# First routing that keeps four sequences' tokens in fifteen slot tiles, and fourteen attention steps moved among the first feed-forward's tiles

## What is computed

```python
x = x + 0.5 * ffn(layernorm(x), Wr, br, W1, b1, W2, b2)
x = x + attn(layernorm(x), wq, wk, wv, wproj, g_rms)
x = x + 0.5 * ffn(layernorm(x), Wr, br, W1, b1, W2, b2)

def ffn(x, Wr, br, W1, b1, W2, b2):        # 8 experts, 128 -> 512 -> 128, top 1
    expert_idx = argmax(xf @ Wr.T + br)
    h = relu(einsum('td,efd->etf', xf, W1) + b1[:, None, :])
    y = einsum('etf,edf->etd', h, W2) + b2[:, None, :]
    return y[expert_idx, arange(tokens)]

def attn(x, wq, wk, wv, wproj, g_rms):     # 16 heads of 8
    q, k, v = x @ wq.T, x @ wk.T, x @ wv.T
    q, k = rope(rms(q)), rope(rms(k))
    return softmax(q @ k.T * scale + 1.0) @ v @ wproj.T
```

## Time and profile before

| | |
|---|---|
| median of 3 runs | 525.54 us (523.85 to 528.15) |
| profiled execution, span of the core | 554.1 us |
| its mean granted TensorE clock | 0.921 of full |
| busy: TensorE, VectorE, ScalarE, GpSimd | 87%, 69%, 61%, 53% |
| first feed-forward in the trace | about 36 to 121 us |
| steps -20 to -7 (up to the first `max_scores`) | about 121 to 147 us |
| steps -6 to -1 | about 147 to 170 us |
| second feed-forward | from about 450 us |

### The profile page before, as it was taken

The page is one execution under the profiler, slowest core; times in us unless marked ns, Lnnn a source line. Parts: engine busy times, 40 slices in busy tenths (PEclk is TensorE's granted clock), DMA queues, the critical chain, the costliest instruction groups (busy, mean ns, idle before and its releaser), DMA issues.

```text
span 554.1 us, 13802 instructions
## 1 busy us (share of the span) xinstructions
PE 480.1 (87%) x4171; PEld 337.8 (61%) x4171; DVE 383.1 (69%) x1047; ACT 340.6 (61%) x765; POOL 291.4 (53%) x408
## 2 busy tenths in 40 slices
PE   7769999996968999999999999989428679979995
PEld 4349999972434555555555555555215348869994
DVE  5836777744786788988888888898117427857773
ACT  4126676632535788888888988867225456536661
POOL 7053455406997677676856665724730503454443
PEclk9989999999885799999999999989657979969999
DMA  7962222111000000000000000000100122123200
GB/s 216 257 239 59 73 70 66 50 30 38 18 18 21 12 7 13 7 11 13 13 7 2 2 4 2 3 1 13 55 25 1 36 53 62 54 66 88 65 29 10
DMA packets 28854, 25.10 MB, mean 45 GB/s; under 512 B 5683, under 2 KB 26074, under 8 KB 28272
## 3 DMA queue, kind: packets, MB, share of 16 engines
q1 hardware_dynamic: 24240, 15.75, 9.7%
q0 software_dynamic: 4544, 8.49, 5.3%
HBM read 14.65 MB, written 10.22 MB: 45 GB/s over the span
## 4 chain that ended last, share of the span: by engine, by line
PE 68%; DVE 13%; issue 6%; another core or an unknown queue 5%; ACT 4%; DMA 2%; POOL 1%; DVEq 1%; SPq 1%; POOLq 0%; ACTq 0%
PE PS L680 13%; PE PS L693 12%; PE PS L822 11%; PE PS L785 10%; DVE Smax L1476 6%; PE PS L770 5%; PE PS L755 4%; PE PS L807 2%; PE PS L852 2%; ACT QkT L909 2%; PE PS L670 1%; PE PS L832 1%; PE PS L840 1%; PE PS L795 1%
## 5 line engine op out<-in xcount | busy, mean ns | idle before, releaser
L1476 DVE TENSOR_REDUCE Smax<-PS 128x4 f32<-128x1024 f32 x128 | 156.2, 1223 | 64.6 <-PE PS L785 49.3
L1010 ACT ACTIVATE Pt<-PS 128x1024 f32<-128x1024 f32 x128 | 128.4, 1033 | 12.6 <-remote 9.4
L680 PE MATMUL PS<-XsT,Ws 128*128 128x128 f32 x624 | 92.4, 293 | 4.1 <-issue 3.3
L693 PE MATMUL PS<-W,HsT 128*128 x624 | 87.5, 285 | 4.0 <-DVE Ys L1371 3.2
L785 PE MATMUL PS<-QkT 24*128 24x256 f32 x512 | 66.0, 336 | 28.8 <-DVE Smax L1476 22.4
L950 ACT ACTIVATE HsT<-PS,Bs 128x128 f32<-128x128 f32 x156 | 48.9, 364 | 64.6 <-PE PS L680 57.6
L680 PEld LDWEIGHTS PS<-XsT,Ws 128*128 128x128 f32 x624 | 79.3, 199 | 8.5 <-issue 4.3
L693 PEld LDWEIGHTS PS<-W,HsT 128*128 128x128 f32 x624 | 78.0, 196 | 7.7 <-issue 6.5
L785 PEld LDWEIGHTS PS<-QkT 24*128 24x128 f32 x512 | 41.9, 198 | 66.4 <-ACT QkT L909 26.9
L822 PE MATMUL PS<-Pt,Vg 128*32 128x256 f32 x1024 | 77.4, 416 | 2.4 <-issue 2.0
L1357 DVE TENSOR_SCALAR HsT<-PS,Bs 128x128 f32<-128x128 f32 x156 | 47.5, 346 | 36.8 <-PE PS L680 34.0
(11 more groups left out here) (190 smaller groups left out, 698.1 us busy)
## 6 DMA issues: line engine op xcount, KB each, us to landing
AtCol<-slots SPq DMA_DIRECT2D x39, 65.5 KB, 1.8
mid<-Ys SPq DMA_DIRECT2D x39, 64.0 KB
rows<-XX SPq DMA_DIRECT2D x8, 288.0 KB, 4.2
XX<-x SPq DMA_DIRECT2D x8, 256.0 KB, 4.6
W<-w1T SPq DMA_DIRECT2D x2, 1024.0 KB, 6.5
W<-w2T SPq DMA_DIRECT2D x2, 1024.0 KB
QkT<-NmaxT SPq DMA_DIRECT2D x64, 4.0 KB
Xs<-rows,TokI POOLq DMA_INDIRECT x39
```

The costliest lines, as they stand in the source:

```text
L680: last = nc.tensor.matmul(PS[:, 2 + 2 * (n % 2) + c // 2, (c % 2) * P:(c % 2 + 1) * P], Ws[:, n % R_WS, c * P:(c + 1) * P], XsT[:, n % 2, ...
L693: last = nc.tensor.matmul(PS[:, y_bank(n), 0:P], HsT[:, n % 2, c, :], W2[:, ds(e * D_FF + c * P, P)], start=(c == 0), stop=(c == FC - 1))
L1010: nc.scalar.activation(Pt[:, m % 2, 2 * pair:2 * pair + 2, :, :].rearrange("p h c t -> p (h c t)"), PS[:, score_bank(m, pair):score_bank(m ...
L1476: nc.vector.tensor_reduce(Smax[:, b % 2, :, at:at + 33:32].rearrange("p t h -> p h t"), PS[:, max_bank(m, pair):max_bank(m, pair) + 2, :]. ...
```

## The change

- **Slots.** The tokens of the first four sequences (token tiles 0 to 7) get slots in the first 15 slot tiles (`SINGLE`): each expert's early tokens are rounded up to whole tiles, the later tokens first fill what is left there, then stand behind tile 14. `totals()` has four products in place of two and waits for a new matrix `After`, which VectorE makes ahead of its `layernorm(0)` once `route_in` is complete. `route()` computes two sets of ends and a jump, and the table of experts compares with 16 ends in place of 8.
- **Stores.** Tiles 0 to 14 are stored to a tensor of their own, `mid_early`, from which tiles 0 to 7 are fetched; behind tile 20 SyncE copies it into `mid`.
- **Steps.** Steps -20 to -7 stand within the loop of the first feed-forward, at the end of the turns that `RAMP` names; so do the two early layernorms, the rope tables and the router's part of `Wp`. GpSimd issues the gather of tile t + 7, then the fetches of `EARLY_LOADS`, then the steps of turn t.
- **PSUM.** From tile 15 on the transposed tile and the result of `down` have one bank each, as the steps need banks 6 and 7.
- **Fetches of the other 24 tiles** start in step -6 rather than in -14; tiles 8 to 11, which `reload(4)` of step -4 needs, are fetched in steps -6 and -5. The fills of steps -18 to -7 are gone.

```diff
+EARLY = 8
+SINGLE = EARLY + N_EXP - 1
+RAMP = {20: (-20,), 21: (-19, -18, -17), 22: (-16,), 23: (-15,), 25: (-14,), 26: (-13,), 28: (-12,), 30: (-11,), 31: (-10,), 33: (-9,),
+        35: (-8,), 37: (-7,)}
+RAMP_END = -6
+LOAD_TILE = 16
+FIRST_NORM, FIRST_INVERSE, SECOND_INVERSE = 18, 19, 20
+TABLES_TILE = 12
+COPY_TILE = SINGLE + 5
+WP_TURN, WP_ROUTER = SINGLE + 1, SINGLE + 2
+EARLY_LOADS = {16: (0, 1), 17: (2,), 18: (3,), 19: (4,), 20: (5,), 21: (6,), 22: (7,)}
...
-HIGH_AT = {-12: 0, -5: 1}
-GATHER_STEP = [-14, -14, -10, -10, -9, -5, -3, -1, -6, -3, -2, 1, 2, 5, 6, 9, 10, 13, 14, 17, 18, 21, 22, 25]
+HIGH_AT = {-10: 0, -5: 1}
+LOW_AT = {-9: 0}
+GATHER_STEP = [-6, -6, -5, -5, -4, -3, -2, -1, 0, 1, 2, 3, 4, 5, 6, 9, 10, 13, 14, 17, 18, 21, 22, 25]
...
+    mid_early = nc.dram_tensor("mid_early", [SINGLE * P, P], F32).ap()
...
-            return n % 2 if n < S_TILES else 0
+            return n % 2 if n < SINGLE else 0
...
-            return 6 + n % 2 if n < S_TILES else 1
+            return 6 + n % 2 if n < SINGLE else 1
...
-                sp.dma_start(mid[s * P:(s + 1) * P, :], Ys[:, s % R_YS, :]).then_inc(y_kept[s % R_YS], 16)
+                sp.dma_start((mid_early if s < SINGLE else mid)[s * P:(s + 1) * P, :],
+                             Ys[:, s % R_YS, :]).then_inc(y_kept[s % R_YS], 16)
+                if s == COPY_TILE:
+                    for u in range(R_YS):
+                        sp.wait_ge(y_kept[u], 16 * count(0, SINGLE - 1, u))
+                    sp.dma_start(mid[0:SINGLE * P, :], mid_early).then_inc(early_copied, 16)
...
+                early = j < EARLY
                 pool.indirect_dma_start(
-                    X[:, j, :], None, mid,
+                    X[:, j, :], None, mid_early if early else mid,
                     bass.IndirectOffsetOnAxis(ap=SlotI[:, j:j + 1], axis=0),
-                    bounds_check=S_TILES * P - 1, oob_is_err=False).then_inc(mid_in[lot(j)], 16)
+                    bounds_check=(SINGLE if early else S_TILES) * P - 1, oob_is_err=False).then_inc(mid_in[lot(j)], 16)
 
...
+            pool.wait_ge(tok_ready, 1)
+            for c in range(N_CHUNK):
+                pool.wait_ge(rows_out[c], 16)
+            for t in range(R_XS):
+                gather(t)
+            for t in range(S_TILES):
+                if t + R_XS < S_TILES:
+                    gather(t + R_XS)
+                if t == LOAD_TILE:
+                    stored(SINGLE)
+                    pool.wait_ge(tables_ready, 1)
+                for j in EARLY_LOADS.get(t, ()):
+                    fetch(j)
+                for n in RAMP.get(t, ()):
+                    step(n)
+            stored(S_TILES)
+            pool.wait_ge(early_copied, 16)
+            for n in range(RAMP_END, END):
+                step(n)
...
-                tot = Seen[:, N_TILES - 1, :]
-                nc.tensor.matmul(PS[:, 3, 0:N_EXP], Before[:], tot, start=True, stop=True)
-                nc.tensor.matmul(PS[:, 3, N_EXP:2 * N_EXP], Ones[:], tot, start=True, stop=True).then_inc(counts_ps, 1)
+                pe.wait_ge(after_ready, 1)
+                early, every = Seen[:, EARLY - 1, :], Seen[:, N_TILES - 1, :]
+                nc.tensor.matmul(PS[:, 3, 0:2 * N_EXP], Ones[:], Seen[:, EARLY - 1:N_TILES:N_TILES - EARLY, :], start=True, stop=True)
+                nc.tensor.matmul(PS[:, 3, 2 * N_EXP:3 * N_EXP], Before[:], early, start=True, stop=True)
+                nc.tensor.matmul(PS[:, 3, 3 * N_EXP:4 * N_EXP], After[:], early, start=True, stop=False)
+                nc.tensor.matmul(PS[:, 3, 3 * N_EXP:4 * N_EXP], Before[:], every, start=False, stop=True).then_inc(counts_ps, 1)
...
-                    if n >= (1 if k else 2):
-                        pe.wait_ge(y_ready, n if k else n - 1)
+                    if n >= SINGLE:
+                        pe.wait_ge(y_ready, n)
+                    elif n >= 2:
+                        pe.wait_ge(y_ready, n - 1)
...
+                    if not k:
+                        if t == WP_TURN:
+                            wp_turn()
+                        if t == WP_ROUTER:
+                            wp_router()
+                        for n in RAMP.get(t, ()):
+                            step(n)
 
...
+                pe.wait_ge(wp_in, 16 * N_HEAD)
+                pe.wait_ge(y_ready, SINGLE)
+                nc.tensor.transpose(PS[:, 7, 0:P], Wp[:, 0:P], I[:]).then_inc(wpT_ps, 1)
+
...
+                        else:
+                            if t == WP_TURN:
+                                act.wait_ge(wpT_ps, 1)
+                                copy(WpT[:], PS[:, 7, 0:P]).then_inc(wpT_ready, 1)
+                            if t == FIRST_INVERSE:
+                                inverse_deviation(1)
+                            if t == SECOND_INVERSE:
+                                inverse_deviation(2)
+                            for n in RAMP.get(t, ()):
+                                step(n)
...
+                if early:
+                    e, l = slice(0, early), slice(early, r.stop)
+                    wide = [P, r.stop - early, N_EXP]
+                    tt_(Place[:, e], Seen[:, e], Base[:].unsqueeze(1).to_broadcast([P, early, N_EXP]), ALU.add)
+                    link(tt_(Place[:, l], Seen[:, l], BaseLate[:].unsqueeze(1).to_broadcast(wide), ALU.add))
+                    link(tt_(Lg[:, l], Place[:, l], Ends[:, 0].unsqueeze(1).to_broadcast(wide), ALU.is_ge))
+                    link(tt_(Lg[:, l], Lg[:, l], Jump[:].unsqueeze(1).to_broadcast(wide), ALU.mult))
+                    link(tt_(Place[:, l], Place[:, l], Lg[:, l], ALU.add))
...
+                link(ts_(PadsI[:].rearrange("p k e -> p (k e)"), PS[:, 3, 0:2 * N_EXP], float(P - 1), None, ALU.add))
+                link(ts_(PadsI[:], PadsI[:], shift, shift, ALU.logical_shift_right, ALU.logical_shift_left))
+                link(nc.vector.tensor_copy(Pads[:], PadsI[:]))
+                link(tt_(Pads[:, 1], Pads[:, 1], Pads[:, 0], ALU.subtract))
+                link(nc.vector.tensor_tensor_scan(Ends[:].rearrange("p k e -> p (k e)"), OneCol[:, 0:2 * N_EXP],
+                                                  Pads[:].rearrange("p k e -> p (k e)"), 0.0, ALU.mult, ALU.add))
+                nc.vector.scalar_tensor_tensor(out=Base[:], in0=Ends[:, 0], scalar=-1.0, in1=Pads[:, 0],
+                                               op0=ALU.add, op1=ALU.subtract)
+                link(tt_(Jump[:], Ends[:, 1], Pads[:, 1], ALU.subtract))
+                tt_(BaseLate[:], Base[:], PS[:, 3, 3 * N_EXP:4 * N_EXP], ALU.add)
+                tt_(Jump[:], Jump[:], Ends[:, 0], ALU.subtract)
+                link(tt_(Base[:], Base[:], PS[:, 3, 2 * N_EXP:3 * N_EXP], ALU.add))
+                link(slot_numbers(every, EARLY))
...
+                wide = [P, S_TILES, 2 * N_EXP]
+                dve.wait_ge(ids_ready, 2)
+                link(tt_(ExpC2, Ends[:].rearrange("p k e -> p (k e)").unsqueeze(1).to_broadcast(wide),
+                         Start[:].unsqueeze(2).to_broadcast(wide), ALU.is_le))
+                link(nc.vector.tensor_reduce(ExpF[:], ExpC2, AX, ALU.add))
+                link(nc.vector.tensor_copy(ExpI[:], ExpF[:]))
+                ts_(ExpI[:], ExpI[:], N_EXP - 1, None, ALU.bitwise_and).then_inc(slots_ready, 1)
...
+                    else:
+                        if t == TABLES_TILE:
+                            rope_tables()
+                        if t == WP_ROUTER:
+                            dve.wait_ge(wpr_ps, 1)
+                            nc.vector.tensor_copy(Wp[:, P:P + N_EXP], PS[:, 7, P:P + N_EXP]).then_inc(wpr_ready, 1)
+                        if t == FIRST_NORM:
+                            reload(1)
+                            layernorm(1)
+                        for n in RAMP.get(t, ()):
+                            step(n)
...
+            link(tt_(After[:], Ones[:], Before[:], ALU.subtract))
+            tt_(After[:], After[:], I[:], ALU.subtract).then_inc(after_ready, 1)
+            layernorm(0)
+            row_shift(0)
```

240 lines of the change are left out of this document (114 added, 126 removed).

## The result

The changed kernel takes **533.86 us** (530.68 to 536.85, 4 runs), the kernel before 524.69 us (523.27 to 528.15, 4 runs): a ratio of 1.013, 95% interval 1.0081 to 1.018, so 4 to 9 us slower. Forecast were 533.9 us and "slower" at 0.63.

The account below looks back on a forecast made before the run. TensorE was taken as full in the first feed-forward, with a 26.5 us chain of waits behind it. -25.6 + 6.8 + 14.1 + 1.1 + 3.0 + 7.0 + 2.0 = +8.4 on 525.5 gives 533.9 us, range 528 to 541.

Parts of the forecast that it names:

- Saved, 25.6: Between last feed-forward output and first max_scores: the 26.5 us chain moves into the feed-forward, leaving 0.9; 25.6 us saved.
- 6.8: First feed-forward: moved projections, transposes, turns and small Wp operations put on a full TensorE, 6.8 us, all paid.
- 14.1: First feed-forward, turns 18, 20 and 23: TensorE stalls because VectorE waits for reloads, 14.1 us in sum, bounds 10 to 18.
- 1.1: First feed-forward, turn 33: sums(1) and low(0) on VectorE, less slack and that turn's transposes, cost 1.1 us.
- 3.0: First feed-forward: granted clock falls to half behind the third wait, costing 3.0 us, bounds 0 to 12.
- The three waits: VectorE waiting for loads ahead of the reloads in turns 18, 20 and 23: 3.9, 2.0 and 4.6 us.
- the three stalls: TensorE held up by late VectorE outputs after the reloads of turns 18, 20 and 23: 4.5, 3.7 and 5.9 us.
- Rival A: Whole kernel: loads are hidden, the feed-forward and ramp waits vanish and the clock stays up; 513.4 us, chance 0.18.
- Ramp, 7.0: Steps -6 to -1: fetches of tiles 8 to 11 stand behind GpSimd's split and rope, so VectorE waits 7.0 us.
- Nothing takes that back: Ramp: the 7.0 us wait is paid in full, since TensorE is nearly full from 163 us on.
- Head, 2.0: Kernel's start: routing makes TokI some 4 us later, partly hidden in the first gather's wait; 2.0 us, bounds 0.6 to 4.0.
- The rule on the two sides of SBUF: GpSimd can't write DMA descriptors during VectorE's two-port modes; loads up to 0.6 us slower per instruction, not seen in trace.

Follow-up runs that it names:

- e11: Changed kernel with GpSimd issuing each turn's fetches ahead of that turn's gather: 561.31 us, ratio 1.011 to the kernel before.
- e2: Changed kernel with the three early reloads and other moved steps in later turns, fetches left in place: 560.28 us, ratio 1.008 to the kernel before.
- e4: Changed kernel keeping slots, mid_early, single banks and Wp work, but steps, early layernorms and fetches back behind the feed-forward: 561.69 us, 1.004 to the kernel before.
- e9: Kernel before with eight more indirect GpSimd DMAs, unused, behind the gathers of tiles 23 to 30: 569.63 us, ratio 1.022 to the kernel before.
- e1: Changed kernel with GpSimd's fetches of tiles 8 to 11 ahead of the split and rope: 566.14 us, ratio 1.018 to the kernel before.
- e3: Changed kernel with the edits of both e1 and e2: 556.29 us, ratio 0.998 to the kernel before.

## Why the prediction was right, point by point

- **Saved, 25.6.** Right: the first max_scores is 0.81 us behind the last output (147.87 to 148.68), for which 0.9 was set.
- **Feed-forward, 6.8 + 14.1 + 1.1 + 3.0 = 25.0.** Measured 110.1 less 83.7, **26.4 us**. The three waits were forecast at 3.9, 2.0 and 4.6 and are 4.20, 1.65 and 4.63. That their cause is the place of the fetches behind the gathers is shown by e11, that they can be had away by e2. The terms of the sum are less exact than the waits. Windows of the feed-forward before, then after, and of two stretches at half clock:

```profile
36.98:120.70 83.72, 82.69 (x663) 79.49 (x663) 58.00 (x234) 52.97 (x153) 33.88 (x34) 0.96 0.23 59
```

```profile
37.74:147.87 110.13, 94.01 (x685) 87.46 (x685) 70.11 (x285) 61.28 (x187) 55.61 (x66) 0.91 0.23 59
84.10:91.00 6.90, 5.11 (x23) 4.82 (x24) 3.88 (x19) 1.92 (x7) 3.15 (x4) 0.51 0.18 49
94.40:97.80 3.40, 3.40 (x16) 3.08 (x15) 1.90 (x8) 1.49 (x5) 1.99 (x2) 0.50 0.93 311
```

  TensorE's idle time is 15.1 us longer (1.0 to 16.1), where 14.1 + 1.1 were forecast. But the three stalls are 4.11, 1.90 and 4.87 us and not 4.5, 3.7 and 5.9, so VectorE had more slack than 0.9, and turns 26 to 38 have about 3 us of idle time and not 1.1. The clock cost twice its 3.0: TensorE works 18.3 us at half and not 5.8, half of the difference is 6.3. The forecast counted the stretch behind the third wait alone and let the ones behind the first two fall into the next wait; the second wait took in some 0.4 us at most (1.65 in place of 2.0), and the fetch of the third stands behind output 22, which the slow work ahead of it makes later too. What is left, 26.4 - 15.1 - 6.3 = 5.0, is the moved work, for which 6.8 were set. So errors of +3.3 and -1.8 stand behind a sum that is off by 1.4. That one result bank costs nothing by itself e4 shows.
- **What the 14.1 left out.** The forecast took it for granted that a fetch costs nothing but the wait for it. On the experiments' chips that is wrong: e9 puts a price of 1.2 us on each fetch between gathers, the clock that falls with it included. In the changed kernel's own trace no such pause of over 0.9 us is seen on ScalarE or VectorE in the feed-forward. On the other chip there are three (the relu of ScalarE stands 2.24, 1.21 and 2.41 us), and still the waits for loads are 10.4 us where they were 10.5, and the feed-forward is 110.3 and 110.1. So there the pauses hide behind the waits, and taking the waits away (e2) gives 6.9 us and not 14. Rival A took them for pure gain; on those chips it would have missed by some 7 us. What e2 would give on the first chip no run shows.
- **Ramp, 7.0.** The wait is 6.68, the loads land 17.25 us behind the first max_scores (forecast 17.1), and the ramp is 7.3 us longer (22.9 to 30.2). "Nothing takes that back" is too strong: the clock came back sooner and returned 1.6 us, and without the wait only 4.3 to 4.7 us come back (e1, e3 against e2): next in line stand VectorE's stretched operation, for 1.5 us, and TensorE at half speed. That the clock gave the 1.6 is argued from the traces' order, not shown by a run of its own. The DMA rows agree with the durations taken from the earlier trace rows: 163.34 to 165.93 is 2.59 us. (The first load's 10.7 should be 10.6 by the numbers that it names.)
- **Head, 2.0.** Mis-sized: `TokI` is 2.65 us later (29.27 to 31.92), the first `Xr` 0.76. The row:

```profile
36.58 0.35 DVE L1416 TENSOR_SCALAR Xr<-Xs 128x128 f32<-128x128 f32 x1 [3.87 <-DMA Xs<-rows,TokI]
```

  VectorE waits 3.87 us where it waited 5.76; more was hidden than the "nearer to the lower" bound allowed for. By its own 4.0 less 3.2 the lower bound is 0.8, not 0.6, and that is what was measured.
- **Sum.** By the trace: head 0.8, feed-forward 26.4, less 25.6, makes 1.5; ramp 7.3; clock -1.6. That is +7.1 us, against +8.4 forecast and +9.2 between the medians, whose interval goes from 4 to 9. Head too dear by 1.2, feed-forward too cheap by 1.4, and within the feed-forward the clock too cheap and the moved work too dear: the mechanism of the waits was right, and part of the hit is luck.
- **The rule on the two sides of SBUF** (the Trainium skill, SBUF — State Buffer, SBUF: two separate sides) was weighed as a danger for GpSimd's DMAs. In the changed kernel's feed-forward it did not come true: the eight fetches take 0.99 or 1.00 us. But "the trace shows no such thing" holds only for the rows that the prediction looked at. In the same trace of before, two fetches that start beside VectorE's `Rn` take 1.56 and 1.39 us, up to the 0.6 us more that it reckoned with:

```profile
141.01 0.69 DVE L1459 TENSOR_TENSOR Rn<-Rot,Rr 128x512 f32<-128x512 f32 x1 [0.88 <-POOL Rot L546]
141.06 1.56 POOL L489 DMA_INDIRECT XX<-mid,SlotI  x1
...
150.00 0.68 DVE L1459 TENSOR_TENSOR Rn<-Rot,Rr 128x512 f32<-128x512 f32 x1
...
150.18 1.39 POOL L489 DMA_INDIRECT XX<-mid,SlotI  x1 [0.30 <-issue]
```

  The page says in the same place that engine ports and DMA ports can't contend, and that TensorE's and ScalarE's ports never wait on anyone. By that no port of SBUF explains what e9 cost, as it is TensorE's semaphore that comes late; no run here shows whether it is a port or something else.
